# A depthwise convolution over four row tiles of 64 rows and one of 32 rows instead of five of 64

## The chip, the cores and the metric

The kernel runs on one core of a Trainium2 chip. The metric is the device time of one execution in microseconds. All arrays are fp32; TensorE works on them as sums of two parts (a leading and a trailing one), since one pass alone is not exact enough.

## The reference

The input is 8 images x 96 channels x 256 x 256. Layer 0 normalises, runs a windowed linear attention with two projections and a batch norm, and is added to its input. Layer 1 is what the change touches:

```python
x = x + _L0_conv_ref(_gn(x), ...)          # attention
x = x + _L1_conv_ref(_gn(x), ...)          # wavelet convolution
# _L1_conv_ref, B, C, H, W = 8, 96, 256, 256
for i in range(3):
    co = haar2d(cur)                       # (B, C, 4, h, w), h = H / 2, H / 4, H / 8
    cur = co[:, :, 0]
    flat = dwconv(flat, wconv_w[i]) * wscale[i]        # 5 x 5, one filter for each channel and band
for i in reversed(range(3)):
    next_ll = ihaar2d(level_coeffs[i] with next_ll added to band 0)
base = dwconv(x, base_w) * base_scale + base_b         # 5 x 5, one filter for each channel
return base + next_ll
```

## The kernel before

The program has three stages: statistics of the first image, the attention, and from about 5570 us on the wavelet convolution, which is the only stage that the change touches (but for a table of filters that the first stage lays down in memory). Its work is cut into 192 groups: 96 channels, and for each channel a first group (images 0 to 3, `g` = 0) and a second one (images 4 to 7, `g` = 1).

In a group the 256 rows of an image are covered by `WINDOWS` = 5 tiles of `WROWS` = 64 rows, of which `OROWS` = 52 are output rows and 4 on each side are halo. A tile uses 128 partitions: 64 rows times two column phases (even and odd columns). The base filter and the first wavelet level are folded into one filter, so that the convolution of a tile is a product with banded matrices `mat1`: `TAPS` = 5 column shifts, each as three matmuls (leading x leading, leading x trailing, trailing x leading; `split`, L1292 to L1294) of 512 columns (4 images x 128). The sum lies in PSUM in `ps_w` of the tile. Levels 2 and 3 work on the half-size image `ll1`, which TensorE sums up from all tiles with `down_sb` (`sum_down`, L1300), and their result `next_a`, `next_b` is added into the tiles' sums with `up_sb` (L1344, L1346).

The order on each engine is written out by hand, and semaphores join them. For group `qn`:

- TensorE: convolution of tiles 0 and 1, level 3 (L1331 to L1334), level 2 (L1292 to L1294 with `in`), convolution of tiles 2, 3 and 4, then, once `next_lo` says that `next_b` is ready, six matmuls that add the upper levels, and at once the ten of `sum_down` for group `qn + 1`.
- ScalarE: copies `ps_ll` to `ll1` (L1263), the leading parts of the inputs of levels 2 and 3 (L1265, L1267), then for group `qn + 1` the normalisation `norm` (L1243, sixteen instructions, split by half of the partitions, phase and image) and `leading` (L1256, L1258: the leading part `zb` of each tile; the first and the last tile go through a mask), then copies `ps_3` and the leading part of the upper levels (L1277, L1278).
- VectorE: `finish` of tile 0 of group `qn - 1` (L1438), `make_in` (L1392, L1395: inputs of levels 2 and 3), `finish` of tile 1, `split_in` (L1402), `finish` of tiles 2 to 4, `make_x1` for group `qn + 2` (L1369: input plus scaled attention output), `trailing` for group `qn + 1` (L1382, L1385: the trailing part of each tile, after `leading` of the same tile), `up_levels` (L1409 to L1419), `split_next` (L1424, L1426).
- GpSimd builds the banded matrices of a channel from the loaded rows: `mat1` (casts L1185, subtractions L1193) as soon as they have landed, and `mat2`, `mat3` when level 2 of the channel before has been done (`l2_ready`).
- SyncE issues all transfers in one queue: the inputs `xb`, `yb` three groups ahead, once `make_x1` has set the buffers free; the outputs, tile by tile; and behind the outputs of a channel's last group the filters `raw1`, `raw2`, `raw3` for the next channel but one, then the next inputs.

## Time and profile before

| | us |
|---|---|
| median of 3 runs | 11053.4 (11053.02 to 11074.61) |
| the profiled execution, its own time | 11061.64 |
| its span, first to last instruction | 11059.8 |
| TensorE busy in the span | 10538.7 (95%) |
| VectorE busy | 9242.7 (84%) |
| ScalarE busy | 7168.6 (65%) |
| GpSimd busy | 3679.7 (33%) |
| mean granted clock of TensorE | 0.992 of full speed |

The share of busy time is an average over three stages. The third stage repeats one pattern of two groups; the page's 40 slices show TensorE at 9 tenths in all of them, VectorE at 7, ScalarE at 5, GpSimd at 2 and the DMA engines at 7. Which engine ends a group is seen only in the timelines of single groups.

### The profile page before, as it was taken

Reading aid. Unit: us, or ns where it says so; the run is one execution under the profiler, and the core shown is the slowest. Engines: PE = TensorE matmul, PEld = TensorE weight load, DVE = VectorE, ACT = ScalarE, POOL = GpSimd, SP = SyncE. Lnnn points to the kernel's source line nnn. Section 1 sums busy time; section 2 is a strip of 40 time slices with the busy share of each in tenths; the row PEclk is TensorE's granted clock in tenths of the full one; section 3 lists DMA queues with packets and bytes.
Section 4 is the critical chain, followed back from the end, with each engine's and each line's share of the span. In section 5 each row is a group of like instructions: output and inputs, shape, how many; then the busy total and the mean of one; then the engine's idle time right before and its main releaser. Section 6 shows DMA issues by size and latency. Waiting matters only on the chain. (4 is left out here: it accounts for less than half of the span.)

```text
span 11059.8 us, 205333 instructions
## 1 busy us (share of the span) xinstructions
PE 10538.7 (95%) x66084; PEld 8946.0 (81%) x66084; DVE 9242.7 (84%) x16479; ACT 7168.6 (65%) x11852; POOL 3679.7 (33%) x3715
## 2 busy tenths in 40 slices
PE   4999999999999999999969999999999999999999
PEld 4888888888888888888858888888888888888887
DVE  6989989899998999988867777777777777777777
ACT  4777777777777777778735555555555555555554
POOL 3444444444444444444322222222222222222222
PEclk9999999999999999999979999999999999999999
DMA  5323333232333333322257777677777767767775
GB/s 185 133 92 126 109 109 126 92 130 95 126 114 104 114 103 115 126 81 74 69 124 154 155 156 154 154 152 155 156 157 157 155 153 156 155 153 154 152 156 125
DMA packets 1162861, 1453.43 MB, mean 131 GB/s; under 512 B 215391, under 2 KB 1125023, under 8 KB 1125279
## 3 DMA queue, kind: packets, MB, share of 16 engines
q1 hardware_dynamic: 1161055, 1442.80, 51.6%
q10 hardware_dynamic: 1376, 6.13, 0.1%
q8 instruction: 119, 1.95, 0.1%
q14 instruction: 311, 2.55, 0.1%
HBM read 1040.11 MB, written 408.56 MB: 131 GB/s over the span
## 5 line engine op out<-in xcount | busy, mean ns | idle before, releaser
L1292 PE MATMUL ps_w<-zb,mat 128*128 128x512 f32 x4800 | 1925.6, 401 | 8.6
L1293 PE MATMUL ps_w<-zb,mat 128*128 128x512 f32 x4800 | 1906.4, 397 | 0.0
L1294 PE MATMUL ps_w<-zb,mat 128*128 128x512 f32 x4800 | 1904.9, 397 | 0.0
L634 POOL CAST xn_hi<-xs 96x512 fp32r<-96x512 f32 x1024 | 840.7, 821 | 3112.3 <-PE ps_qkv L659 2261.1
L1438 DVE SCALAR_TENSOR_TENSOR ob<-ps_w,prm,x 64x512 f32<-64x512 f32 x1920 | 1440.5, 750 | 515.6 <-PE ps_w L1344 476.8
L1243 ACT ACTIVATE z<-x,prm 64x384 f32<-64x384 f32 (+1 forms) x3072 | 1814.0, 662 | 58.8 <-DVE x L1369 51.1
L1185 POOL CAST mat<-raw 128x1280 fp32r<-128x1280 f32 (+1 forms) x288 | 464.7, 1631 | 3947.6 <-DMA raw<-vec 2351.3
L657 PE MATMUL ps_qkv<-wqkv_hi,xn_hi 96*128 96x288 f32 x4096 | 1388.9, 339 | 38.2 <-POOL xn_lo L636 19.9
L636 POOL TENSOR_TENSOR xn_lo<-xs,xn_hi 96x512 fp32r<-96x512 f32 x1024 | 1363.4, 1331 | 81.8
L658 PE MATMUL ps_qkv<-wqkv_lo,xn_hi 96*128 96x288 f32 x4096 | 1214.1, 296 | 0.0
L659 PE MATMUL ps_qkv<-wqkv_hi,xn_lo 96*128 96x288 f32 x4096 | 1211.8, 296 | 0.0
L584 ACT ACTIVATE tok<-ps_qkv 128x1152 f32<-128x1152 f32 x1024 | 1160.6, 1133 | 0.0
L1292 PEld LDWEIGHTS ps_w<-zb,mat 128*128 128x128 f32 x4800 | 903.0, 188 | 302.9 <-DVE ob L1438 91.0
L552 ACT ACTIVATE att<-ps_t 96x512 f32<-96x512 f32 x1024 | 608.1, 594 | 805.2 <-PE ps_t L702 805.2
L687 PE MATMUL ps_g<-tok 128*104 128x97 f32 x8192 | 947.2, 259 | 160.2 <-DVE tok L795 160.1
L1294 PEld LDWEIGHTS ps_w<-zb,mat 128*128 128x128 f32 x4800 | 901.7, 188 | 227.0
L1293 PEld LDWEIGHTS ps_w<-zb,mat 128*128 128x128 f32 x4800 | 901.6, 188 | 209.3
L679 PE MATMUL ps_num<-kv_sb,q_sb 104*128 104x104 f32 x8192 | 1062.8, 273 | 0.0
L695 PE MATMUL ps_f<-att,wp_sb 96*96 96x512 f32 x2048 | 1052.6, 594 | 6.9 <-DVE f_cur_b L176 3.1
L679 PEld LDWEIGHTS ps_num<-kv_sb,q_sb 104*128 104x128 f32 x8192 | 1018.1, 192 | 0.0
L687 PEld LDWEIGHTS ps_g<-tok 128*104 128x104 f32 x8192 | 833.6, 172 | 222.4 <-DVE tok L795 219.7
L1263 ACT ACTIVATE ll<-ps_ll 128x512 f32<-128x512 f32 x192 | 114.8, 598 | 1373.4 <-PE ps_ll L1300 1373.4
(196 smaller groups left out, 24154.1 us busy)
## 6 DMA issues: line engine op xcount, KB each, us to landing
xst<-in_x SPq DMA_DIRECT2D x96, 2048.0 KB, 13.8
xs<-in_x SPq DMA_DIRECT2D x128, 1536.0 KB, 8.9
y_scratch<-ys SPq DMA_DIRECT2D x128, 1536.0 KB, 9.5
out<-ob SPq DMA_DIRECT2D x768, 208.0 KB
xb<-in_x SPq DMA_DIRECT2D x576, 256.0 KB
yb<-y_scratch SPq DMA_DIRECT2D x576, 256.0 KB
raw<-vec SPq DMA_DIRECT2D x192, 320.0 KB, 4.2
raw<-vec SPq DMA_DIRECT2D x384, 160.0 KB, 3.9
```

The costliest lines, as they stand in the source:

```text
L584: s_.activation(tok[:, slot].rearrange("p g (t c) -> p g t c", t=3)[:, :, :, 0:C], ps_qkv[:, :, 0:3 * C].rearrange("p g (t c) -> p g t c", ...
L636: nc.gpsimd.tensor_tensor(lo, pixels(xs, k, j), hi.bitcast(F32), ALU.subtract).then_inc(xlo_ready, 1)
L657: mm(o, hi, wqkv_hi[:], start=True, stop=False)
L658: mm(o, hi, wqkv_lo[:], start=False, stop=False)
L659: last = mm(o, lo, wqkv_hi[:], start=False, stop=True)
L679: last = mm(ps_num[:, g, 0:QR], q_sb[:, slot, g * 128:(g + 1) * 128], kv_sb[:, g // 2, :], start=True, stop=True)
L687: last = mm(ps_g[0:QR, w * GW:(w + 1) * GW], tok[:, slot, g, PART:PART + QR], tok[:, slot, g, 2 * PART:2 * PART + GW], start=g % 2 == 0, s ...
L1243: last = nc.scalar.activation(z[q * WROWS:(q + 1) * WROWS, ts, b, :], x1[slot(k, g)][rows, pairs, b, q::2], ACT.Identity, scale=prm[k][row ...
L1292: mm(out_, w[HI], xx[HI], start=start, stop=False)
L1293: mm(out_, w[HI], xx[LO], start=False, stop=False)
L1294: return mm(out_, w[LO], xx[HI], start=False, stop=stop)
L1438: last = v.scalar_tensor_tensor(out=ob[p:p + WROWS, t // 2].rearrange("p b w -> p (b w)")[:, q::2], in0=ps_w[t][q * WROWS:(q + 1) * WROWS, ...
```

## The change

The five tiles are laid out anew. Four of them (0 to 3) still have 64 rows and two column phases. The tile with number `SPECIAL` = 4 has `SROWS` = 32 rows, of which 24 are output rows, and four column phases (`SPHASES`), so that it uses 128 partitions too, with a quarter of the columns (`BLOCKS` = 64 an image). Its convolution needs `STAPS` = 3 shifts instead of 5, and 256 columns instead of 512. It has a matrix of its own, `mat_s`, built from `raw_s`, which eight more DMAs load for each channel, and buffers of its own: `x1_s` (the four slots side by side in the partitions), `zn`, `zq`, `zs`. ScalarE normalises its 32 rows into `zn` and then moves each of the four phases into its partitions of `zq`. The other tiles now all lie inside the image, so the masks are gone. `sum_down` writes the half-size image in another order of columns (even ones first). The constants `down_sb` and `up_sb` are made on VectorE instead of being loaded, and only the borders of the padded buffers are set to zero, for which SyncE no longer waits.

```diff
-NV1 = 4 * TAPS * 2
+NV1 = 4 * (TAPS + 2) * 2
...
+SROWS = WROWS // 2
+SPHASES = 128 // SROWS
+STAPS = 3
+BLOCKS = W // SPHASES
+SPECIAL = WINDOWS - 1
+TILES = ((0, 0, WROWS - HALO), (WROWS - 2 * HALO, HALO, WROWS - 2 * HALO),
+         (H - 2 * WROWS + 2 * HALO, HALO, WROWS - 2 * HALO), (H - WROWS, HALO, WROWS - HALO),
+         (2 * WROWS - 4 * HALO, HALO, SROWS - 2 * HALO))
+
+
+def tile_place(t):
+
+    return (t % 2) * WROWS, t // 2, SROWS if t == SPECIAL else WROWS
...
-                                full = p1[:, ia, q, :, o, first:first + 2 * TAPS - 1:2]
+                                full = p1[:, ia, q, 1:1 + TAPS, o, first:first + 2 * TAPS - 1:2]
...
-            x1 = [sb_(f"x1_{s}", [128, PAIRW, IMGS, W]) for s in range(SLOTS)]
+            x1 = [sb_(f"x1_{s}", [128, SPECIAL // 2, IMGS, W]) for s in range(SLOTS)]
+            x1_s = sb_("x1_s", [SLOTS * SROWS, IMGS, W])
             xb = sb_("xb", [128, PAIRW, IMGS, W])
             yb = sb_("yb", [128, PAIRW, IMGS, W])
             ob = sb_("ob", [128, PAIRW, IMGS, W])
-            zb = [[sbr_(f"zb{g}_{h}", [128, WINDOWS, IMGS, ZW]) for h in range(2)] for g in range(SETS)]
+            zb = [[sbr_(f"zb{g}_{h}", [128, SPECIAL, IMGS, ZW]) for h in range(2)] for g in range(SETS)]
+            zs = [[sbr_(f"zs{g}_{h}", [128, IMGS, BLOCKS + 2]) for h in range(2)] for g in range(SETS)]
...
+            raw_s = sb_("raw_s", [128, SPHASES * STAPS, SROWS])
...
+            mat_s = [[sbr_(f"mat_s{k}_{h}", [128, STAPS, 128]) for h in range(2)] for k in range(2)]
...
+            zn = sb_("zn", [SROWS, IMGS, W])
+            zq = sb_("zq", [128, IMGS, BLOCKS])
+            ll1 = sb_("ll1", [128, 2, IMGS, HALF // 2])
...
-            NRAW = (4 + 2 + 4) * 16
+            NRAW = (4 + 8 + 2 + 4) * 16
...
-                for t_ in (xb, yb, *zb[0], *zb[1], *in2_p, in3_hl):
-                    eng.memset(t_[:].bitcast(F32), 0.0).then_inc(zeroed, 1)
-                eng.memset(zero1[:], 0.0).then_inc(zeroed, 1)
-
-            N_ZERO = 2 + 2 * SETS + 3 + 1
-
-            down_raw = ob[:, 0].rearrange("p b w -> p (b w)")[:, 0:WINDOWS * HALF].rearrange("p (t w) -> p t w", t=WINDOWS)
-            up_raw = ob[:, 1].rearrange("p b w -> p (b w)")[:, 0:WINDOWS * HALF].rearrange("p (t w) -> p t w", t=WINDOWS)
+                for t_, n, width in padded_tiles:
+                    for at in (slice(0, n), slice(width - n, width)):
+                        eng.memset(t_[:].bitcast(F32)[..., at], 0.0).then_inc(zeroed, 1)
+
+            N_ZERO = 2 * len(padded_tiles)
+            N_SET = 5 + (SPECIAL + 2) + 2 * (2 * 2 * 2 + 2 * SPHASES)
+            UPPER_AT, LOWER_AT = {0: 0, 1: 1, SPECIAL: 2}, {SPECIAL: 4, 2: 6, 3: 7}
...
-                for dst, src in ((down_raw, down), (up_raw, up), (inside_sb[:], inside)):
-                    sp.dma_start(dst, src).then_inc(const_in, 16)
...
+                    for ia in range(2):
+                        for q in range(SPHASES):
+                            first = q * SROWS + ia
+                            sp.dma_start(raw_s[first:first + SROWS - 1:2, :, :],
+                                         bass.AP(tensor=vec1.tensor,
+                                                 offset=c * (NV1 * V1) + (((2 * ia + q % 2) * (2 * TAPS + 4) + q // 2 * 2) * V1
+                                                                          + (2 + WROWS - SROWS)),
+                                                 ap=[[2, SROWS // 2], [V1, SPHASES * STAPS], [1, SROWS]])).then_inc(raw_in, 16)
...
-                sp.wait_ge(zeroed, N_ZERO)
...
-                        build([(mat1[k], raw1[:].rearrange("p (d o) m -> p d (o m)", o=2)[:, :, ::-1], "p d m -> p d m")],
+                        build([(mat1[k], raw1[:].rearrange("p (d o) m -> p d (o m)", o=2)[:, :, ::-1], "p d m -> p d m"),
+                               (mat_s[k], raw_s[:].rearrange("p (d o) m -> p d (o m)", o=SPHASES)[:, :, ::-1],
+                                "p d m -> p d m")],
...
+                    for b in range(IMGS):
+                        img = IMGS * g + b
+                        last = nc.scalar.activation(
+                            zn[:, b], x1_s[own(k, g), b], ACT.Identity,
+                            scale=prm[k][own(k, g), 2 + img:3 + img], bias=prm[k][own(k, g), 2 + B + img:3 + B + img])
+                    last.then_inc(zn_set, 1)
                     for p in range(2):
-                        ts = slice(p, WINDOWS, 2)
-                        pairs = slice(0, len(range(p, WINDOWS, 2)))
+                        ts = slice(p, SPECIAL, 2)
+                        pairs = slice(0, SPECIAL // 2)
                         rows = slice(p * WROWS, (p + 1) * WROWS)
...
+                    act.wait_ge(zn_set, m * 4 + (2 * k + g + 1))
+                    for q in range(SPHASES):
+                        last = nc.scalar.activation(zq[q * SROWS:(q + 1) * SROWS].rearrange("p b j -> p (b j)"),
+                                                    zn[:].rearrange("p b w -> p (b w)")[:, q::SPHASES], ACT.Copy)
                     last.then_inc(z_set, 1)
 
                 def leading(qn, g):
                     act.wait_ge(z_set, qn + 1)
-                    for t in range(WINDOWS):
-                        o = zb[g][HI][:, t, :, 2:2 + HALF]
-                        i = z[:, t]
-                        if t in EDGES:
-                            e = EDGES[t]
-                            nc.scalar.activation(o, i, ACT.Identity, scale=mask[:, e:e + 1], bias=zero1[:]).then_inc(z_hi, 1)
-                        else:
-                            nc.scalar.activation(o, i, ACT.Copy).then_inc(z_hi, 1)
+                    for t in range(SPECIAL):
+                        nc.scalar.activation(zb[g][HI][:, t, :, 2:2 + HALF], z[:, t], ACT.Copy).then_inc(z_hi, 1)
+                    nc.scalar.activation(zs[g][HI][:, :, 1:1 + BLOCKS], zq[:], ACT.Copy).then_inc(z_hi, 1)
...
+                    for t in range(SPECIAL):
                         for h in (HI, LO):
-                            last = mm(ps_ll[:], down_sb[:, t, :], zb[g][h][:, t, :, 2:2 + HALF], start=t + h == 0,
-                                      stop=t + h == WINDOWS)
+                            mm(ps_ll[:], down_sb[:, t, :],
+                               zb[g][h][:, t, :, 2:2 + HALF].rearrange("p b (j v) -> p v b j", v=2), start=t + h == 0, stop=False)
+                    for v in range(2):
+                        for h in (HI, LO):
+                            last = mm(ps_ll[:, v * HALF * 2:(v + 1) * HALF * 2], down_sb[:, SPECIAL + v, :], zs[g][h][:, :, 1:1 + BLOCKS], start=False,
+                                      stop=v + h == 2)
                     last.then_inc(ll_ready, 1)
...
+                        if t == SPECIAL:
+                            for d in range(STAPS):
+                                split(ps_w[t][:, 0:IMGS * BLOCKS], [mat_s[k][h][:, d, :] for h in range(2)],
+                                      [zs[g][h][:, :, d:d + BLOCKS] for h in range(2)], d == 0, False)
+                            return
...
+                        for at, half in ((UPPER_AT, next_a), (LOWER_AT, next_b)):
+                            if t == SPECIAL:
+                                for v in range(2):
+                                    last = mm(ps_w[t][:, 0:IMGS * BLOCKS], up_sb[:, at[t] + v, :], half[:, v::2], start=False,
+                                              stop=half is next_b and v == 1)
+                            elif t in at:
+                                last = mm(ps_w[t][:], up_sb[:, at[t], :], half[:], start=False, stop=True)
                         last.then_inc(win_ready, 1)
...
-                        n = 128 if 2 * i + 1 < WINDOWS else WROWS
-                        v.scalar_tensor_tensor(out=x1[slot(k, g)][0:n, i].rearrange("p b w -> p (b w)"),
+                        n = 128 if i < SPECIAL // 2 else SROWS
+                        to = x1[slot(k, g)][:, i] if i < SPECIAL // 2 else x1_s[own(k, g)]
+                        v.scalar_tensor_tensor(out=to.rearrange("p b w -> p (b w)"),
...
-                        o = zb[g][LO][:, t, :, 2:2 + HALF]
-                        hi = zb[g][HI][:, t, :, 2:2 + HALF].bitcast(F32)
-                        if t in EDGES:
-                            e = EDGES[t]
-                            last = v.scalar_tensor_tensor(out=o, in0=z[:, t], scalar=mask[:, e:e + 1], in1=hi,
-                                                          op0=ALU.mult, op1=ALU.subtract)
+                        if t == SPECIAL:
+                            inner = [zs[g][h][:, :, 1:1 + BLOCKS] for h in range(2)]
                         else:
-                            last = v.tensor_tensor(o, z[:, t], hi, ALU.subtract)
-                        last.then_inc(z_lo, 1)
+                            inner = [zb[g][h][:, t, :, 2:2 + HALF] for h in range(2)]
+                        v.tensor_tensor(inner[LO], zq[:] if t == SPECIAL else z[:, t], inner[HI].bitcast(F32), ALU.subtract
...
-                        v.tensor_tensor(in2[:, s], ll1[:, :, 0::2], ll1[:, :, 1::2], op).then_inc(in2_ready, 1)
+                        v.tensor_tensor(in2[:, s], ll1[:, 0], ll1[:, 1], op).then_inc(in2_ready, 1)
...
+                        for q in range(SPHASES if t == SPECIAL else 0):
+                            last = v.scalar_tensor_tensor(
+                                out=ob[0:SROWS, t // 2].rearrange("p b w -> p (b w)")[:, q::SPHASES],
+                                in0=ps_w[t][q * SROWS:(q + 1) * SROWS, 0:IMGS * BLOCKS], scalar=prm[k][own(k, g), 1:2],
+                                in1=x1_s[own(k, g)].rearrange("p b w -> p (b w)")[:, q::SPHASES],
+                                op0=ALU.add, op1=ALU.add)
+                        for q in range(0 if t == SPECIAL else 2):
```

ScalarE, one group in the middle of the third stage: from the copy of `ps_ll` to that of the upper levels. Before:

```order
L1263 ACTIVATE ll1<-ps_ll 128x512
L1265 ACTIVATE in2_0<-in2 128x8x64
L1267 ACTIVATE in3_hl<-in3 128x8x32
L1243 ACTIVATE z<-x1_2,prm_1 64x3x128 x8
L1243 ACTIVATE z<-x1_2,prm_1 64x2x128 x8
L1256 ACTIVATE zb0_0<-z,zero1,mask 128x4x128
L1258 ACTIVATE zb0_0<-z 128x4x128 x3
L1256 ACTIVATE zb0_0<-z,zero1,mask 128x4x128
L1273 ACTIVATE s3<-ps_3 128x512
L1277 ACTIVATE next_a<-next_ll 64x512
L1278 ACTIVATE next_b<-next_ll 64x512
```

and now:

```order
L1298 ACTIVATE ll1<-ps_ll 128x512
L1300 ACTIVATE in2_0<-in2 128x8x64
L1302 ACTIVATE in3_hl<-in3 128x8x32
L1268 ACTIVATE zn<-x1_s,prm_1 32x256 x4
L1279 ACTIVATE z<-x1_2,prm_1 64x2x128 x16
L1285 ACTIVATE zq<-zn 32x256 x4
L1292 ACTIVATE zb0_0<-z 128x4x128 x4
L1293 ACTIVATE zs0_0<-zq 128x4x64
L1308 ACTIVATE s3<-ps_3 128x512
L1312 ACTIVATE next_a<-next_ll 64x512
L1313 ACTIVATE next_b<-next_ll 64x512
```

The sixteen instructions of `norm` are still there, all in the smaller form; four stand ahead of them and four behind them, and `leading` follows.

GpSimd, the matrices of one channel. Before:

```order
L1185 CAST mat1_1_0<-raw1 128x640
L1187 REGISTER_ALU
L1193 TENSOR_TENSOR mat1_1_1<-raw1,mat1_1_0 128x256 x2
L1193 TENSOR_TENSOR mat1_1_1<-raw1,mat1_1_0 128x128
L1205 REGISTER_ALU
L1185 CAST mat2_0<-raw2 128x1280
L1185 CAST mat3_0<-raw3 128x1280
L1193 TENSOR_TENSOR mat2_1<-raw2,mat2_0 128x256 x5
L1193 TENSOR_TENSOR mat3_1<-raw3,mat3_0 128x256 x5
```

and now (tile names as in the program, with the number of the channel's buffer):

```order
L1215 CAST mat1_1_0<-raw1 128x640
L1215 CAST mat_s1_0<-raw_s 128x384
L1217 REGISTER_ALU
L1223 TENSOR_TENSOR mat1_1_1<-raw1,mat1_1_0 128x256 x2
L1223 TENSOR_TENSOR mat1_1_1<-raw1,mat1_1_0 128x128
L1223 TENSOR_TENSOR mat_s1_1<-raw_s,mat_s1_0 128x256
L1223 TENSOR_TENSOR mat_s1_1<-raw_s,mat_s1_0 128x128
L1237 REGISTER_ALU
L1215 CAST mat2_0<-raw2 128x1280
L1215 CAST mat3_0<-raw3 128x1280
L1223 TENSOR_TENSOR mat2_1<-raw2,mat2_0 128x256 x5
L1223 TENSOR_TENSOR mat3_1<-raw3,mat3_0 128x256 x5
```

A cast and two subtractions for `mat_s` have come in, between the matrix `mat1` and the matrices `mat2` and `mat3`.

SyncE's queue, the filters of one channel, four kinds of DMA with their counts, now:

```order
L1133 DMA raw1<-vec1 32x10x64 x4
L1140 DMA raw_s<-vec1 16x12x32 x8
L1146 DMA raw2<-vec2 64x10x128 x2
L1150 DMA raw3<-vec3 32x10x128 x4
```

The second line is new; the inputs `xb` and `yb` of the next group to be loaded are issued behind these.

## Rows read from the trace of the kernel before

**Rows 1.** Timeline of TensorE: start us, us busy, instruction, shape, count.

```profile
8038.00 0.39 PE L1292 MATMUL ps_w<-zb,mat 128*128 128x512 f32 x1
...
8041.28 0.39 PE L1294 MATMUL ps_w<-zb,mat 128*128 128x512 f32 x1
...
8047.73 0.28 PE L1292 MATMUL ps<-in,mat 128*128 128x256 f32 x1
...
8051.40 0.39 PE L1292 MATMUL ps_w<-zb,mat 128*128 128x512 f32 x1
...
8090.32 0.86 PE L1344 MATMUL ps_w<-next_a,up_sb 128*128 128x512 f32 x3
```

**Rows 2.** Timeline of ScalarE, 8040 to 8045 us.

```profile
8040.16 0.41 ACT L1267 ACTIVATE in_hl<-in 128x256 fp32r<-128x256 f32 x1
8040.47 5.19 ACT L1243 ACTIVATE z<-x,prm 64x384 f32<-64x384 f32 x8
```

**Rows 3.** Timeline of ScalarE, 8034 to 8096 us; idle time and releaser in brackets.

```profile
8038.20 0.60 ACT L1263 ACTIVATE ll<-ps_ll 128x512 f32<-128x512 f32 x1 [8.35 <-PE ps_ll L1300]
...
8066.52 0.60 ACT L1263 ACTIVATE ll<-ps_ll 128x512 f32<-128x512 f32 x1 [5.88 <-PE ps_ll L1300]
...
8068.80 9.50 ACT L1243 ACTIVATE z<-x,prm 64x384 f32<-64x384 f32 x16
8078.34 0.82 ACT L1256 ACTIVATE zb<-z,zero,mask 128x512 fp32r<-128x512 f32 x1
8079.06 1.66 ACT L1258 ACTIVATE zb<-z 128x512 fp32r<-128x512 f32 x3
...
8094.29 0.60 ACT L1263 ACTIVATE ll<-ps_ll 128x512 f32<-128x512 f32 x1 [8.38 <-PE ps_ll L1300]
```

**Rows 4.** Timeline of VectorE, first group of a channel.

```profile
8075.62 3.66 DVE L1369 SCALAR_TENSOR_TENSOR x<-yb,gain,xb 128x1024 f32<-128x1024 f32 x3
8079.20 0.74 DVE L1382 SCALAR_TENSOR_TENSOR zb<-z,mask,zb 128x512 fp32r<-128x512 f32 x1
8079.87 1.88 DVE L1385 TENSOR_TENSOR zb<-z,zb 128x512 fp32r<-128x512 f32 x3
8081.68 0.74 DVE L1382 SCALAR_TENSOR_TENSOR zb<-z,mask,zb 128x512 fp32r<-128x512 f32 x1
...
8085.99 0.69 DVE L1426 TENSOR_TENSOR next_b<-next_ll,next_b 64x512 fp32r<-64x512 f32 x1
```

**Rows 5.** Timeline of VectorE, second group of a channel.

```profile
8050.87 0.74 DVE L1382 SCALAR_TENSOR_TENSOR zb<-z,mask,zb 128x512 fp32r<-128x512 f32 x1
...
8053.34 1.75 DVE L1382 SCALAR_TENSOR_TENSOR zb<-z,mask,zb 128x512 fp32r<-128x512 f32 x1
...
8061.24 1.13 DVE L1426 TENSOR_TENSOR next_b<-next_ll,next_b 64x512 fp32r<-64x512 f32 x1
```

**Rows 6.** Timeline of GpSimd over the same two groups.

```profile
8051.73 4.48 POOL L1185 CAST mat<-raw 128x1280 fp32r<-128x1280 f32 x2 [17.42 <-PE ps L1294]
8056.39 7.95 POOL L1193 TENSOR_TENSOR mat<-raw,mat 128x256 fp32r<-128x256 f32 x10 [0.18 <-POOL mat L1185]
8087.84 0.72 POOL L1185 CAST mat<-raw 128x640 fp32r<-128x640 f32 x1 [23.50 <-DMA raw<-vec]
```

**Rows 7.** Timeline of SyncE's queue: issues of DMAs.

```profile
8076.94 3.02 SPq L1111 DMA_DIRECT2D raw<-vec  x4
...
8084.81 0.36 SPq L1130 DMA_DIRECT2D xb<-in_x  x1
```

**Rows 8.** Windows: stretch, its length, busy us of PE, PEld, DVE, ACT, POOL (instructions), clock, DMA share, GB/s.

```profile
1480.00:1484.00 4.00, 0.69 (x5) 0.47 (x4) 1.45 (x4) 1.22 (x3) 0.00 (x0) 0.86 0.06 14
1484.00:1487.30 3.30, 3.30 (x16) 3.26 (x16) 0.98 (x2) 0.32 (x1) 0.00 (x0) 0.50 0.00 0
...
8100.00:8101.00 1.00, 1.00 (x6) 0.77 (x6) 0.97 (x2) 1.00 (x2) 0.00 (x0) 1.00 0.31 108
```

**Rows 9.** Timeline of GpSimd, and of SyncE's queue, where the third stage begins.

```profile
5569.57 2.66 POOL L1075 MEMSET xb<- 128x3072 f32 x1 [69.52 <-POOLq L885]
...
5586.53 2.73 SPq L1111 DMA_DIRECT2D raw<-vec  x4
```

More of the change, by code:

```diff
@@ new lines, in _ @@
+                dve.wait_ge(down_set, 5)
+                for t, (start, skip, n) in enumerate(TILES):
+                    to = slice((start + skip) // 2, (start + skip + n) // 2)
+                    for v_ in range(2 if t == SPECIAL else 1):
+                        first = skip // 2 + v_ * (SROWS // 2)
+                        v.tensor_scalar(down_sb[:, t + v_, to], pair_sums[:, t // SPECIAL, first:first + n // 2], 0.5, None,
+                                        ALU.mult).then_inc(down_set, 1)
@@ new lines, in _ @@
+                for rows, at in ((0, UPPER_AT), (64, LOWER_AT)):
+                    for t in at:
+                        start, skip, n = TILES[t]
+                        width = tile_place(t)[2]
+                        src = ident_sb[rows:rows + 64, (start + skip) // 2:(start + skip + n) // 2]
+                        for q in range(128 // width):
+                            which = at[t] + (q // 2 if t == SPECIAL else 0)
+                            for to in (0, 64):
+                                o = up_sb[to:to + 64, which, q * width + skip:q * width + skip + n]
+                                v.tensor_scalar(o.rearrange("p (a r) -> p a r", r=2), src.unsqueeze(2).to_broadcast(
+                                    [64, n // 2, 2]), 0.5, None, ALU.mult).then_inc(down_set, 1)
```

86 lines of the change are left out of this document (40 added, 46 removed).

## The prediction

> **What bounds the kernel now.** The page puts TensorE at 95%, which would make it the bound. I read the timelines of the single engines over the two groups of one channel, since the shares cannot tell who is late at the end of a group. Each group is measured from the copy of `ps_ll` on ScalarE (L1263), which I call T0: 8038.20 for a second group, 8066.52 for the next first group, 8094.29 for the one after [rows 3]. So a second group takes 28.32 us and a first group 27.77, and the pair 56.09.
>
> In the first group TensorE ends it. VectorE has `next_b` ready at 8085.99 + 0.69 = 8086.68, T0 + 20.16 [rows 4], and TensorE comes to the upper levels only at 8090.32, T0 + 23.80 [rows 1]. VectorE is 3.6 us early. In the second group VectorE ends it: `next_b` is ready at 8061.24 + 1.13 = 8062.37, T0 + 24.17 [rows 5], later than TensorE's 23.8. From there six matmuls, `sum_down` and the semaphores take 4.15 us to the next T0.
>
> Why does VectorE take 4 us more in the second group? From the start of `trailing` to the end of `next_b` it needs 7.48 us in the first group (8079.20 to 8086.68) and 11.50 in the second (8050.87 to 8062.37) [rows 4, 5]. The work is the same, but GpSimd builds `mat2` and `mat3` meanwhile, from 8051.73 to 8064.34 [rows 6]; the same instruction on the last tile takes 0.74 us in the one group and 1.75 in the other. The Trainium skill (SBUF — State Buffer, "Who interferes with whom") says that a VectorE instruction with two SBUF inputs and a GpSimd instruction that reads SBUF exclude one another for their whole length, and that the one which starts second is blocked. These two rows agree with it.
>
> The third near tie is ScalarE. In the first group `norm` runs from 8068.80 for 9.50 us and the first leading part is there at 8078.34 + 0.82 = 8079.16 [rows 3]. VectorE comes out of `make_x1` and starts `trailing` at 8079.20 [rows 4]. There is no slack at all between them.
>
> **TensorE saves.** Fifteen matmuls of 512 columns in tile 4 become nine of 256. The pace is (8041.28 - 8038.00) / 14 = 0.234 us for the large and (8051.40 - 8047.73) / 30 = 0.122 for the small ones [rows 1]: 3.51 - 1.10 = 2.41 us a group. The columns of the upper levels and of `sum_down` stay the same in sum. TensorE would now be ready at T0 + 21.39. What `sum_down` pays for reading every second column no row shows; the bounds are nothing and a doubling of eight matmuls (1.9 us a group, on the path in both groups). I take nothing, since the elements moved are as many.
>
> **ScalarE pays.** The larger form of `norm` costs 5.19 / 8 = 0.65 us, the smaller one (9.50 - 5.19) / 8 = 0.54 [rows 2, 3]. Sixteen small ones make 8.62. Four for `zn` at the small form's price, which has the same per-partition scale and as many elements, make 2.16 (bounds 0.41 and 0.54 each). Four for `zq`, plain copies of 256 elements, are nearest to L1267's 0.41 [rows 2]: 1.64 (0.54 each as the upper bound). `norm` is then 12.42 us, 2.92 more. The first leading part becomes a plain copy, 1.66 / 3 = 0.55 and about 0.2 cheaper than the masked one with its overlap [rows 3]. So `trailing` can start 2.72 us later than now, at T0 + 15.40 instead of T0 + 12.68. The copies for `zq` read every fourth fp32. By the same page of the Trainium skill (its note on cachelines) a stride of two still hits a 16-byte line twice and a stride of four does not, so that `zq` should cost extra; no row here shows it.
>
> **VectorE.** `finish` of tile 4 gets four instructions of 256 instead of two of 512; each has a fixed part, and I reckon 0.5 us more. That lies ahead of `make_x1` and under ScalarE's delay. `trailing` gets four at 0.6 and one at half of that, 2.74 us instead of 3.14 (the two masked ones 0.67 each): 0.40 less [rows 4]. From `trailing` to `next_b` it is 7.48 - 0.40 = 7.08.
>
> **First group.** `next_b` at 15.40 + 7.08 = T0 + 22.48, later than TensorE's 21.39. VectorE's chain takes over, and of TensorE's 2.41 us only a part comes through: 22.48 + 4.15 = 26.63, against 27.77 now: -1.14.
>
> **Second group.** Here four things come together.
> 1. GpSimd's matrices start at the end of level 2, T0 + 13.5 (8051.73 - 8038.20), and last 12.6 us [rows 6]. Now `trailing` starts 0.9 us ahead of the first cast (8050.87), so that its first four tiles run free, and the excess is 4.0 us in all [rows 5]. Then it will start 1.9 us after the first cast, and all ten instructions with two SBUF inputs meet GpSimd. I reckon 4.5 (bounds 4.0, as now, and 6.0: ten times the 0.5 to 0.6 which the later ones lose, plus half a cast).
> 2. The filters. Eight DMAs of 192 short rows stand in SyncE's queue between the old ones and the inputs. An issue takes 0.36 to 0.76 us [rows 7]; at 0.55 that is 4.4 us. The matrices `mat1` started at 8087.84, T0 + 21.3 of the first group, while VectorE stood idle [rows 6]. They will start near T0 + 26 and, with `mat_s`, lie over `make_in` of the second group, which delays ScalarE's start as well. The inputs are issued from 8084.81 [rows 7] and the DMA engines were busy with them up to about 8100 [rows 8], T0 + 5.7 of the second group; `make_x1` wants them at T0 + 9.1 (as 8075.62 in rows 4). They will land near T0 + 11.6. `make_x1` then ends near T0 + 15 or 16. For both together I take 1.0 us (bounds 0 and 1.7).
> 3. `next_b` comes at 15.40 + 1.0 + 7.08 + 4.5 = T0 + 27.98. TensorE, ready at 21.4 to 23, stands idle for 5 us or more.
> 4. In the attention stage TensorE was busy for 0.69 of 4.0 us (1480 to 1484), and the granted clock in the next 3.3 us of full work was 0.50, the 1.2 GHz level [rows 8]. So the upper levels and `sum_down`, which end the path, can run at half pace: nothing to 3 us, and I take 1.5. The Trainium skill (TensorE: Matmul & The Clock Gate, "HAM oscillation") warns of idle gaps in each round of a loop in the same sense.
>
> Sum: 15.40 + 1.0 + 7.08 + 4.5 + 4.15 + 1.5 = 33.63 against 28.32: +5.31.
>
> **Sum.** The pair costs 5.31 - 1.14 = +4.17 us, times 96 channels = +400. At the start of the stage SyncE no longer waits for the memsets (from 5569.57 to 5586.53 [rows 9]), 17.0 us, less 4.4 for the new issues: -12. The constants made on VectorE lie beside this load. Together +388. Against the profiled execution's 11061.6 that is 11450; the median of the runs lies 8.2 us below it, so I forecast 11441, rounded to 11440.
>
> **The rivals.**
> - *Data come in time and the clock holds.* Then the second group is 15.40 + 7.08 + 4.5 + 4.15 = 31.1, +2.8, the pair +1.7, with the start +150: 11200. With the cheapest ends (4.0 for GpSimd, `zn` at 0.41) it is about +60. For it: 5 us of idle may miss the clock. Chance 0.22.
> - *The inputs come so late that `make_x1` runs under GpSimd's casts.* Its three instructions of 1.2 us have two SBUF inputs each; at the 1.0 us that a blocked one lost [rows 5] the second group gets 3 us more: +288, 11730. Strided reads of `sum_down` would add in the same range (1.9 x 192 = 365). For it: the inputs' landing at T0 + 11.6 is only 2 us ahead of the casts. Chance 0.14.
> - *Faster: ScalarE's delay is swallowed in the second group.* If GpSimd and VectorE, after the shift, exclude one another no longer than now and the new eight small ScalarE instructions cost half of my price (0.24 each), the second group stays near 28.3 and the first gains 2.4: -230 - 12, 10810. It decides at a second group of under 29.5 us. Against it: 0.41 is the cheapest 256-element instruction in these rows. Chance 0.12.
> - *No change.* The losses and gains cancel between these. Chance 0.04.
>
> **How the numbers follow.** My forecast, VectorE's chain late in both groups with the clock falling in the second, has 0.48. The range leaves out the faster case and the far half of the late inputs: 11090 to 11720. For a change of under 0.2% (22 us) a measurement of this kernel cannot tell it from none. Slower: 0.48 + 0.22 + 0.14 = 0.84, of which 0.01 goes to the middle for the cheapest ends; same 0.05; faster 0.12.
>
> **What the profile after would show.** TensorE's matmuls of tile 4 at 0.12; `norm` of 24 instructions at 12.4 us; VectorE waiting 2 us for ScalarE ahead of `trailing` in both groups, where it waited for nothing; T0 distances near 26.6 and 33.6; GpSimd's `mat1` cast after the next T0; the clock below 1.0 every 60 us. I am wrong if ScalarE's new instructions are cheap, if VectorE is in time under GpSimd, or if the clock stays full.

## The result, and the profile after

The changed kernel takes 11952.8 us (median of 4; 11946.8 to 11959.9) against 11053.7 before: ratio 1.081, 95% interval 1.079 to 1.083. It is slower, as forecast, but by 899 us instead of 387, and outside the range. The profiled execution has a span of 11954.6 us, and 0.955 as TensorE's mean granted clock instead of 0.992.

The page of the changed kernel, engines' busy time:

```profile
PE 10633.6 (89%) x65700; PEld 8937.1 (75%) x65700; DVE 9509.9 (80%) x16897; ACT 7811.3 (65%) x13388; POOL 3825.1 (32%) x4015
```

TensorE has 384 matmuls fewer and is busy for 95 us longer, and its share falls from 95% to 89%. So its busy time did not fall with the number of matmuls and columns.

ScalarE's timeline of the two groups, which answers to [rows 3]; a second group is 8035.35 to 8071.01, a first one 8071.01 to 8101.05:

```profile
8035.35 0.60 ACT L1298 ACTIVATE ll<-ps_ll 128x512 f32<-128x512 f32 x1 [7.10 <-PE ps_ll L1338]
...
8071.01 0.60 ACT L1298 ACTIVATE ll<-ps_ll 128x512 f32<-128x512 f32 x1 [7.97 <-PE ps_ll L1338]
...
8073.41 2.06 ACT L1268 ACTIVATE zn<-x_s,prm 32x256 f32<-32x256 f32 x4
8075.50 8.59 ACT L1279 ACTIVATE z<-x,prm 64x256 f32<-64x256 f32 x16
8084.10 2.67 ACT L1285 ACTIVATE zq<-zn 32x256 f32<-32x256 f32 x4
8086.80 2.20 ACT L1292 ACTIVATE zb<-z 128x512 fp32r<-128x512 f32 x4
...
8101.05 0.60 ACT L1298 ACTIVATE ll<-ps_ll 128x512 f32<-128x512 f32 x1 [7.26 <-PE ps_ll L1338]
```

The pair takes 65.70 us; it took 56.09. (Averages over all 96 channels are in the table at the end of the experiments; this pair is typical of them.) `norm` is 2.06 + 8.59 + 2.67 = 13.3 us, and the four copies for `zq` take 0.67 each, half as much again as my 0.41.

VectorE in the first group [rows 4] and, below the gap of the timeline, in the second [rows 5]:

```profile
8078.67 2.72 DVE L1480 SCALAR_TENSOR_TENSOR ob<-ps_w,prm,x_s 32x256 f32<-32x256 f32 x4
...
8083.82 1.27 DVE L1414 SCALAR_TENSOR_TENSOR x_s<-yb,gain,xb 32x1024 f32<-32x1024 f32 x1
8087.47 2.50 DVE L1427 TENSOR_TENSOR zb<-z,zb 128x512 fp32r<-128x512 f32 x4 [2.38 <-ACT zb L1292]
...
8093.88 0.69 DVE L1468 TENSOR_TENSOR next_b<-next_ll,next_b 64x512 fp32r<-64x512 f32 x1
```

```profile
8035.98 1.30 DVE L1434 TENSOR_TENSOR in<-ll 128x256 f32<-128x256 f32 x2 [4.70 <-ACT ll L1298]
8037.31 1.18 DVE L1437 TENSOR_TENSOR in<-in 128x128 f32<-128x128 f32 x2
...
8053.08 4.12 DVE L1427 TENSOR_TENSOR zb<-z,zb 128x512 fp32r<-128x512 f32 x4 [2.44 <-ACT zb L1292]
...
8063.11 0.69 DVE L1468 TENSOR_TENSOR next_b<-next_ll,next_b 64x512 fp32r<-64x512 f32 x1
```

In both groups `trailing` (L1427) now waits 2.4 us for ScalarE (L1292). `finish` of the special tile (L1480) takes 2.7 us. In the second group `make_in` takes 1.30 and 1.18 us where the first has 0.76 and 0.49, since GpSimd's `mat1` and `mat_s` lie over it, and `trailing` takes 4.12 us instead of 2.50 under GpSimd's casts and subtractions. GpSimd's timeline, which answers to [rows 6]:

```profile
8033.97 0.72 POOL L1215 CAST mat<-raw 128x640 fp32r<-128x640 f32 x1 [37.15 <-DMA raw<-vec]
8034.63 0.51 POOL L1215 CAST mat_s<-raw_s 128x384 fp32r<-128x384 f32 x1
...
8050.09 2.87 POOL L1215 CAST mat<-raw 128x1280 fp32r<-128x1280 f32 x2 [11.29 <-PE ps L1328]
8053.15 9.21 POOL L1223 TENSOR_TENSOR mat<-raw,mat 128x256 fp32r<-128x256 f32 x10 [0.18 <-POOL mat L1215]
```

TensorE, from the upper levels to the end of `sum_down` (L1334), second group and first group, which answers to the last of [rows 1]:

```profile
8063.86 1.22 PE L1391 MATMUL ps_w<-next_a,up_sb 128*128 128x512 f32 x2 [5.78 <-DVE next_b L1468]
...
8066.65 3.83 PE L1334 MATMUL ps_ll<-zb,down_sb 128*128 128x512 f32 x8
```

```profile
8094.62 0.73 PE L1391 MATMUL ps_w<-next_a,up_sb 128*128 128x512 f32 x2 [2.09 <-DVE next_b L1468]
...
8096.71 3.82 PE L1334 MATMUL ps_ll<-zb,down_sb 128*128 128x512 f32 x8
```

TensorE waits 5.8 us for VectorE in the second and 2.1 in the first group. The eight matmuls of `sum_down` then take 3.65 us to the start of the next row of work (8066.65 to 8070.30, 8096.71 to 8100.35), 0.456 each. In the kernel before, the ten of the same size took 2.37 us (8091.72 to 8094.09), 0.237 each:

```profile
8091.72 2.53 PE L1300 MATMUL ps_ll<-zb,down_sb 128*128 128x512 f32 x10
```

The windows show what TensorE was granted there (columns as in [rows 8]):

```profile
8064.00:8067.00 3.00, 3.00 (x9) 2.58 (x10) 1.50 (x2) 0.00 (x0) 0.00 (x0) 0.50 0.00 0
8067.00:8071.00 4.00, 4.00 (x13) 2.39 (x12) 0.00 (x0) 0.00 (x0) 0.00 (x0) 0.86 0.22 61
8095.00:8098.00 3.00, 3.00 (x11) 2.46 (x10) 1.50 (x2) 0.00 (x0) 0.00 (x0) 0.58 1.08 302
8098.00:8101.00 3.00, 3.00 (x11) 1.89 (x10) 0.00 (x0) 0.00 (x0) 0.80 (x2) 0.85 0.99 223
```

The clock had fallen in both groups, even after the gap of 2.1 us. (Over the stage it was low at the end of every second group and of two first groups in three.) So these windows cannot say whether `sum_down` is slow for its stride or for the clock. Over the whole stage the trace leans to the stride: the large matmuls of `sum_down` that lie wholly in stretches of full clock take 0.456 us as well. What each costs, the experiments say.

Step by step, in us (T0 is the copy of `ps_ll`):

| | forecast, first | measured | forecast, second | measured |
|---|---|---|---|---|
| T0 to the start of `trailing` | 15.40 | 16.46 | 16.40 | 17.73 |
| to the end of `next_b` | 7.08 | 7.10 | 11.58 | 10.72 |
| to the next T0 | 4.15 | 6.48 | 5.65 | 7.21 |
| group | 26.63 | 30.04 | 33.63 | 35.66 |

### The profile page after: what moved, and what is told of

It is laid out like the page before. It is cut to its first block, busy times and chain, and to the rows that moved or that the text cites. A ratio compares the mean times of both kernels' runs of the same rounds, so it can differ in the third digit from the quotient of the medians.

```text
span 11954.6 us, 209320 instructions
## 1 busy us (share of the span) xinstructions
PE 10633.6 (89%) x65700; PEld 8937.1 (75%) x65700; DVE 9509.9 (80%) x16897; ACT 7811.3 (65%) x13388; POOL 3825.1 (32%) x4015
## 4 chain that ended last, share of the span: by engine, by line
ACT 24%; DVE 13%; PE 11%; issue 5%; SPq 0%; DMA 0%; DVEq 0%; ACTq 0%
ACT z L1279 13%; PE ps_ll L1334 6%; ACT zq L1285 4%; DVE zb L1427 4%; ACT zn L1268 3%; PE ps_w L1391 3%; PE ps_w L1388 1%; DVE in L1434 1%; ACT zb L1292 1%; DVE next_b L1468 1%; DVE next_a L1466 1%; ACT next_a L1312 1%; DVE sum L1451 1%; ACT ll L1298 1%; DVE zs L1427 1%
## 5 line engine op out<-in xcount | busy, mean ns | idle before, releaser
L1215 POOL CAST mat<-raw 128x1280 fp32r<-128x1280 f32 (+1 forms) x288 | 348.0, 1226 | 4686.6 <-DMA raw<-vec 3597.9
L1326 PE MATMUL ps_w<-zb,mat 128*128 128x512 f32 x3840 | 1550.9, 404 | 132.1 <-DVE ob L1486 128.6
L1279 ACT ACTIVATE z<-x,prm 64x256 f32<-64x256 f32 x3072 | 1640.8, 605 | 11.5
L1328 PE MATMUL ps_w<-zb,mat 128*128 128x512 f32 x3840 | 1531.0, 399 | 0.0
L1327 PE MATMUL ps_w<-zb,mat 128*128 128x512 f32 x3840 | 1530.9, 399 | 0.0
L1486 DVE SCALAR_TENSOR_TENSOR ob<-ps_w,prm,x 64x512 f32<-64x512 f32 x1536 | 1152.6, 750 | 203.4 <-PE ps_w L1391 173.7
L1223 POOL TENSOR_TENSOR mat<-raw,mat 128x256 fp32r<-128x256 f32 (+1 forms) x1248 | 1070.4, 891 | 34.7 <-POOL mat_s L1215 17.4
L1326 PEld LDWEIGHTS ps_w<-zb,mat 128*128 128x128 f32 x3840 | 725.2, 189 | 371.6 <-DVE ob L1486 214.1
L1427 DVE TENSOR_TENSOR zb<-z,zb 128x512 fp32r<-128x512 f32 x768 | 648.3, 905 | 437.2 <-ACT zb L1292 437.2
```

What stands on the lines that cost most here:

```text
L1279: last = nc.scalar.activation(z[q * WROWS:(q + 1) * WROWS, ts, b, :], x1[slot(k, g)][rows, pairs, b, q::2], ACT.Identity, scale=prm[k][row ...
L1326: mm(out_, w[HI], xx[HI], start=start, stop=False)
L1327: mm(out_, w[HI], xx[LO], start=False, stop=False)
L1328: return mm(out_, w[LO], xx[HI], start=False, stop=stop)
L1427: v.tensor_tensor(inner[LO], zq[:] if t == SPECIAL else z[:, t], inner[HI].bitcast(F32), ALU.subtract).then_inc(z_lo, 1)
```

## The experiments

Four theories stood after the result: the stride of `sum_down`; the clock fallen in the gaps; ScalarE's longer `norm`; the new filters. They are not exclusive; the question is what each costs, and whether they add up.

**e1: sum_down without a stride.**

```diff
-   zb[g][h][:, t, :, 2:2 + HALF].rearrange("p b (j v) -> p v b j", v=2)
+   zb[g][h][:, t, :, 2:2 + HALF]
```

> The changed kernel with the eight large matmuls of sum_down reading zb in the order in which it lies, as before the change, and ll1 with interleaved columns again. The four small matmuls of the special tile still write their 256 columns side by side, so that they add into the wrong columns: this leaves the special tile's share of the half-size image out of place. Theory 1 (a moving operand with every second fp32 is read at half the pace): the pace goes from 0.46 us a matmul back to 0.24, 1.8 us less a group on the path that ends both groups, 192 groups: about -340 us, 11610. Theory 2 (these matmuls are slow only because TensorE's clock has fallen in the gap ahead of them): the pace stays near 0.46 in the window at the 1.2 GHz level and the time stays near 11950.

Measured: 11742.6 us, -210. TensorE, first group:

```profile
8015.42 0.73 PE L1390 MATMUL ps_w<-next_a,up_sb 128*128 128x512 f32 x2 [2.10 <-DVE next_b L1467]
...
8017.36 3.33 PE L1334 MATMUL ps_ll<-zb,down_sb 128*128 128x512 f32 x8
```

The eight take 3.17 us up to 8020.53, 0.40 each: not 0.24, though the stride is gone. Their clock was 0.63 of full speed (8018 to 8021). Neither theory holds alone. Over the whole stage the large matmuls of e1 take 0.238 us where the clock is full and 0.427 where it is at its low level, 0.33 on average; (0.456 - 0.33) x 8 x 192 = 194 us is nearly all of the 210.

**e2: the stride alone, in the kernel before.**

```diff
-   zb[g][h][:, t, :, 2:2 + HALF]
+   zb[g][h][:, t, :, 2:2 + HALF].rearrange("p b (j v) -> p v b j", v=2)
```

> The kernel before with one part of the change alone: sum_down reads every second column (all ten matmuls), ps_ll and ll1 have the even columns first. Theory 1 (stride halves the pace): ten matmuls at 0.46 instead of 0.24, +2.2 us in each group, 192 groups: +420 us, 11475. Theory 2 (the fallen clock): there is no gap of more than 1 us in this kernel, so the pace stays 0.24 and the time 11055.

Measured: 11479.6 us, +432 against 11047.5 (ratio 1.039, 1.037 to 1.041). The same matmuls, and the window over them:

```profile
8011.38 4.72 PE L1300 MATMUL ps_ll<-zb,down_sb 128*128 128x512 f32 x10
```

```profile
8011.40:8016.00 4.60, 4.60 (x12) 2.11 (x11) 0.62 (x1) 0.00 (x0) 0.40 (x1) 1.00 0.34 77
```

Ten matmuls run 4.6 us at a clock of 1.00. Reading every second fp32 takes nearly twice the time, with the clock at its full level. This part of the change alone costs 4% of the old kernel. The new read also goes in rows of 64 elements, but that is not the cause: the small matmuls of `sum_down` in the changed kernel read rows of 64 side by side at 0.12 us for 256 columns, while those of the upper levels, whose only peculiarity is the step of two (`half[:, v::2]`), take 0.22 to 0.24.

**e3: the copies for zq without their stride.**

```diff
-   zn[:].rearrange("p b w -> p (b w)")[:, q::SPHASES]
+   zn[:].rearrange("p b w -> p (b w)")[:, q * W:(q + 1) * W]
```

> The changed kernel with the four copies into zq reading 256 contiguous elements instead of every fourth: this leaves the phases of the special tile unseparated. Theory: the stride of 16 bytes makes each copy 0.67 us instead of about 0.41, ScalarE's norm is on the path in both groups, so 1.0 us less a group, 192 groups: -200 us, 11750. Rival: the cost is that of a small copy on 32 partitions whatever its stride, or ScalarE is not on the path: 11950.

Measured: 11819.1 us, -134, where the forecast was -200.

```profile
8010.98 0.60 ACT L1298 ACTIVATE ll<-ps_ll 128x512 f32<-128x512 f32 x1 [7.97 <-PE ps_ll L1338]
...
8024.10 1.70 ACT L1285 ACTIVATE zq<-zn 32x256 f32<-32x256 f32 x4
...
8039.94 0.60 ACT L1298 ACTIVATE ll<-ps_ll 128x512 f32<-128x512 f32 x1 [7.11 <-PE ps_ll L1338]
```

The copies take 0.43 each, as forecast for the contiguous form, and the first group falls from 30.04 to 28.96. That is the whole 1.0 us. The rest of the gain, 134 / 96 - 1.1 = 0.3 us, is the second group's. There `trailing` starts 1.0 us earlier too (T0 + 16.7 instead of 17.7 on average), but it still starts behind GpSimd's first cast and takes longer, so that `next_b` is ready only 0.2 us earlier.

**e4: the filters once.**

```diff
-   load_raw(c): raw1 x4, raw_s x8, raw2 x2, raw3 x4; build([mat1, mat_s])
+   load_raw(c): raw1 x4, raw2 x2, raw3 x4; build([mat1]); raw_s and mat_s ahead of the loop
```

> The changed kernel with raw_s loaded once, for channel 0, and mat_s built once into both buffers: this leaves out the special tile's own filter for all other channels, and with it the eight DMAs and the GpSimd work for each channel. Theory (both delay the second group: the matrices are built over make_in, which is blocked for 1.3 us, and the inputs land late): second group about 1.3 us shorter, 96 times: -125 us, 11830; more, -200, if the shorter gap also keeps the clock up. Rival (hidden behind ScalarE and its norm): within 30 us of 11950.

Measured: 11861.2 us, -92. `make_in` of the second group is back at 0.76 and 0.49:

```profile
7998.69 0.76 DVE L1439 TENSOR_TENSOR in<-ll 128x256 f32<-128x256 f32 x2 [4.71 <-ACT ll L1302]
7999.49 0.49 DVE L1442 TENSOR_TENSOR in<-in 128x128 f32<-128x128 f32 x2
```

That is 1.2 us, and 92 / 96 = 0.96 us is what comes out. The forecast was 125 us: the theory holds in size for the second group, which is 1.4 us shorter on average, and misses that the first becomes 0.4 us longer. There GpSimd's cast of `mat1`, no longer delayed by the eight DMAs, now lies over `split_next`:

```profile
8054.99 0.96 POOL L1216 CAST mat<-raw 128x640 fp32r<-128x640 f32 x1 [31.14 <-DMA raw<-vec]
```

```profile
8055.38 1.11 DVE L1473 TENSOR_TENSOR next_b<-next_ll,next_b 64x512 fp32r<-64x512 f32 x1
```

The second of these took 0.69 us in the changed kernel.

**e5 and e6: TensorE kept busy in its gap**, without and with the stride.

```diff
+   for _ in range(7 if g == 0 else 20):     # ahead of pe.wait_ge(next_lo, qn + 1)
+       mm(ps_w[SPECIAL][:, IMGS * BLOCKS:], down_sb[:, 0, :], zb[g][HI][:, 0, 0:2, 2:2 + HALF], start=False, stop=False)
+       mm(ps_w[SPECIAL][:, IMGS * BLOCKS:], down_sb[:, 0, :], zb[g][HI][:, 0, 2:4, 2:2 + HALF], start=False, stop=False)
```

> The kernel of e1 (sum_down reading without a stride; the special tile's share of the half-size image out of place), and the wait of TensorE ahead of the upper levels filled with matmuls whose result nobody reads: 14 of 256 columns in a first group (1.7 us), 40 in a second one (5.0 us). Theory (e1 gained only 210 of the 340 us because the clock had fallen in the gap, where a large matmul takes 0.4 to 0.45 us with or without a stride): the clock stays at full speed, sum_down runs at 0.24, the time from next_b to the next copy of ps_ll falls from 5.9 and 6.3 us to about 4.6 in both groups: -2.9 us a pair, 96 pairs, -280 us against e1, 11460. Rival (e1's pace is held down by something else than the clock, or the fillers only delay): 11740 or more.

> The changed kernel with the same fillers, the strided sum_down left in. Theory (stride and fallen clock each bring a matmul to about 0.45 us, and do not add up): sum_down stays at 0.46, only the six matmuls of the upper levels gain, 0.5 us in a first and 1.0 to 1.3 in a second group: -100 to -170 us, about 11820. Rival (they add up): the gain is as large as in e5, -280, 11670.

Measured: e5 11576.7 us (mean clock 0.989), e6 11863.2 us (0.992). `sum_down` in e5 and in e6, both in windows at a clock of 1.00:

```profile
8024.56 2.09 PE L1334 MATMUL ps_ll<-zb,down_sb 128*128 128x512 f32 x8
```

```profile
8028.50 3.83 PE L1334 MATMUL ps_ll<-zb,down_sb 128*128 128x512 f32 x8
```

The four kernels make a table (us):

| | stride | no stride |
|---|---|---|
| clock falls | 11953 | 11743 (e1) |
| clock held | 11863 (e6) | 11577 (e5) |

Holding the clock gains 90 us with the stride and 166 without; taking the stride away gains 210 with the fallen clock and 286 with the full one. A matmul of 512 columns takes 0.456 us when it is strided (e6, full clock), 0.427 when it runs at the 1.2 GHz level (e1) and 0.456 when it is both (the changed kernel). The two do not add up, so each hides a part of the other. Together they are 376 us. In e6 the clock was full at the end of every group; in e5 it was still low at the end of one second group in five, so that the 166 and 286 are a little small. My expectation for e5 (11460) was too low by 117. The time from `next_b` to the next T0 did fall to 4.6 us in the first groups, as forecast, and to 4.9 in the second; but the 5.9 and 6.3 us of e1 that I started from were those of a single pair, and its averages are 5.3 and 6.1. In both kernels the four small matmuls of the upper levels read `half[:, v::2]`, and stay at 0.22 to 0.24 us instead of 0.12.

**e7 and e8: the upper levels ahead of trailing**, with and without the stride.

```diff
-   make_x1; trailing(qn + 1); up_levels(qn); split_next(qn)         # VectorE
+   make_x1; up_levels(qn); split_next(qn); trailing(qn + 1)
-   norm(qn + 1); leading(qn + 1); copy of ps_3; next_a, next_b      # ScalarE
+   norm(qn + 1), the copy of ps_3 in its middle; next_a, next_b; leading(qn + 1)
```

> The changed kernel, complete and with its strided sum_down, in another order: ScalarE copies ps_3 in the middle of norm and the upper levels' leading parts before leading, VectorE does up_levels and split_next before trailing. Theory (VectorE's wait for ScalarE's longer norm, 2.4 us in both groups, is the start of the loss, and the work behind it need not wait for it): TensorE finds next_b ready and ends the first group, 21.4 + 1.9 + 4.5 = 27.8 us instead of 30.0; the second is ended by trailing at about 27, then sum_down: 31.5 instead of 35.7. [...] -6.3 us a pair: -600 us, 11350. Rival (ScalarE's chain as a whole is the bound, whatever the order): less than 150 us gained, 11800.

> e7 with the unstrided sum_down of e1 (the special tile's share of the half-size image out of place): what the new tiles would give if the reads had no stride. Theory: since the clock now stays up, the whole 1.8 us a group comes back: -340 us against e7, about 11010, level with the kernel before. Rival (something else ends the groups by then): less than 150 us less than e7.

Measured: e7 11534.2 us, -419 where -600 was forecast; e8 11277.8 us, where 11010 was. e7 computes the whole of the reference; e8, like e1, leaves the special tile's share of the half-size image out of place. In e7 the first group is 27.55 us:

```profile
8033.22 0.60 ACT L1300 ACTIVATE ll<-ps_ll 128x512 f32<-128x512 f32 x1 [8.38 <-PE ps_ll L1346]
...
8060.77 0.60 ACT L1300 ACTIVATE ll<-ps_ll 128x512 f32<-128x512 f32 x1 [6.39 <-PE ps_ll L1346]
```

The forecast was 27.8 for it, and 31.5 for the second. That one takes 33.9, and there VectorE waits for something that it had not waited for:

```profile
8012.09 2.48 DVE L1422 SCALAR_TENSOR_TENSOR x<-yb,gain,xb 128x1024 f32<-128x1024 f32 x2 [0.98 <-DMA yb<-y_scratch]
8014.60 2.16 DVE L1422 SCALAR_TENSOR_TENSOR x_s<-yb,gain,xb 32x1024 f32<-32x1024 f32 x1
```

```profile
8028.81 3.48 DVE L1421 SCALAR_TENSOR_TENSOR x<-yb,gain,xb 128x1024 f32<-128x1024 f32 x2 [3.91 <-DMA yb<-y_scratch]
```

`make_x1` waits for its inputs, 0.98 us in e7 and 3.91 in e8. They stand behind the filters in SyncE's queue, and `make_x1` then runs under GpSimd's casts (2.16 us for the third instruction instead of 1.27). The rival with late inputs, which did not show in the changed kernel, appears as the rest gets faster: `make_x1` waits for its inputs in 27 second groups of e1 and 62 of e5, mostly hidden behind ScalarE, and in nearly all of them in e7 and e8. That the filters cause it is not shown alone. What speaks for it is e10 below, which loads them once: its first groups are as short as those of e8, and `make_x1` of its second groups starts at T0 + 10.4 on average, against 14.5 in e8.

The clock did not stay up either, as the expectation for e8 had it: it was low at the end of every second group of e7 and e8. The stride's 1.8 us come back in the first groups of e8 (27.6 to 25.8), and 0.8 us in the second (33.8 to 33.0). The 256 us between e7 and e8 lie between the theory (340) and the rival (under 150).

**e9: the same order in the kernel before.**

```diff
-   make_x1; trailing(qn + 1); up_levels(qn); split_next(qn)         # VectorE
+   make_x1; up_levels(qn); split_next(qn); trailing(qn + 1)
-   norm(qn + 1); leading(qn + 1); copy of ps_3; next_a, next_b      # ScalarE
+   norm(qn + 1); copy of ps_3; next_a, next_b; leading(qn + 1)
```

> The kernel before, complete, in the order of e7: ScalarE copies ps_3 right behind norm and the upper levels' leading parts before leading, VectorE does up_levels and split_next before trailing. Theory (in the kernel before only the second group is ended by VectorE, by 0.4 us; the upper levels' six matmuls would then lie beside trailing): first group unchanged at 27.8 us, second 0.1 to 0.4 shorter: -10 to -40 us, about 11030. Rival (VectorE's work as a whole, blocked by GpSimd, ends the group whatever the order, and leading now starts later): same or up to 50 us slower.

Measured: 10981.1 us against 11061.9 (ratio 0.993, 0.991 to 0.994), the best complete kernel of the study. The rival is refuted: both groups are now ended by TensorE, 27.77 and 27.79 us. The gain is twice the upper end of the theory's 10 to 40 us.

```profile
8003.54 0.60 ACT L1263 ACTIVATE ll<-ps_ll 128x512 f32<-128x512 f32 x1 [8.36 <-PE ps_ll L1305]
...
8031.31 0.60 ACT L1263 ACTIVATE ll<-ps_ll 128x512 f32<-128x512 f32 x1 [8.40 <-PE ps_ll L1305]
...
8059.10 0.60 ACT L1263 ACTIVATE ll<-ps_ll 128x512 f32<-128x512 f32 x1 [8.42 <-PE ps_ll L1305]
```

The second group of the prediction's rows was 28.32, but that one was short for its kind: over the 96 channels of the same trace they run from 28.3 to 29.4 us and average 28.61, the first ones 27.74. In e9 both average 27.76, so that 0.85 x 96 = 82 us a kernel is the whole gain. `next_b` is ready at T0 + 24.5 on average in those second groups, not at the 24.2 of the one pair.

**e10 and e11: what is left without ScalarE's work for the special tile, and then without three of four instructions in finish.** Both stand on `sum_down` without its stride and on filters loaded once. e10 also has 24 small matmuls ahead of TensorE's wait in each second group, as in e5; e11 has none.

```diff
-   4 x zn, 4 x zq for each group
+   4 x zn, 4 x zq for the very first group of the kernel only                # e10, e11
-   for q in range(SPHASES if t == SPECIAL else 0):
+   for q in range(1 if t == SPECIAL else 0):                                 # e11
```

> The changed kernel without stride in sum_down, filters loaded once, 24 filler matmuls of 256 columns in a second group alone, and without the eight ScalarE instructions for zn and zq (the special tile of every group works on the numbers of the first one). Theory (with ScalarE no longer late, trailing starts behind make_x1 at T0 + 14.1, since finish of the special tile takes 2.7 us instead of 1.5): first group ended by TensorE near 26.0 us (27.8 before the change); second near 31.0 (28.3), since trailing starts behind GpSimd's first cast instead of ahead of it: 11150. Rival (VectorE's blocking by GpSimd does not depend on when trailing starts): second near 29.5, 11000.

> e10 without the fillers, and with one instruction instead of four in finish of the special tile (three quarters of that tile's output are left out). Theory: trailing starts at T0 + 12.1, ahead of GpSimd's first cast as before the change, VectorE loses 4 us again and not 5 or 6, and has next_b ready at T0 + 23.2: second group 27.8, first 25.9: 10850. Rival (the place of trailing against GpSimd does not matter): only the 2.0 us of VectorE's work in the second group, -190 us against e10.

Measured: e10 11253.7 us (forecast 11150), e11 10869.3 us (forecast 10850). `trailing` in a second group of e10, in a first one of e10, and in a second one of e11:

```profile
8013.99 5.58 DVE L1438 TENSOR_TENSOR zb<-z,zb 128x512 fp32r<-128x512 f32 x4
...
8046.39 2.48 DVE L1438 TENSOR_TENSOR zb<-z,zb 128x512 fp32r<-128x512 f32 x4
```

```profile
8012.36 3.55 DVE L1433 TENSOR_TENSOR zb<-z,zb 128x512 fp32r<-128x512 f32 x4
```

In e10 the first group is 25.8 us, ended by TensorE, and there the fewer columns show at last: 1.9 us less than before the change, the 2.4 us less what the strided matmuls of the upper levels cost (it is 28.16 in e5, with the same `sum_down` and ScalarE's work). The second is 32.5, worse than my 31.0: `trailing` starts at T0 + 14.1, behind the start of GpSimd's casts, and its four large instructions take 5.6 us instead of 2.5. With 2.05 us less in `finish` it starts at T0 + 12.2, ahead of the casts, and takes 3.6. e11 gains 385 us, or 4.0 a pair, from 2.05 us less on VectorE in a second group (the first is held by TensorE). On average `trailing` starts 2.06 us earlier and the way from there to `next_b` is 1.6 us shorter. The 24 small matmuls are no part of it: they end 2.5 us before `next_b` is ready in e10. The rival, 190, is out: where `trailing` meets GpSimd doubles the price of being late.

The average length of the groups over the 96 channels, in us, from the traces:

| | first | second |
|---|---|---|
| before | 27.74 | 28.61 |
| after | 30.10 | 35.74 |
| e1 | 28.89 | 34.78 |
| e2 | 29.94 | 30.82 |
| e3 | 28.95 | 35.50 |
| e4 | 30.45 | 34.37 |
| e5 | 28.16 | 33.69 |
| e6 | 29.92 | 34.91 |
| e7 | 27.61 | 33.82 |
| e8 | 25.80 | 32.98 |
| e9 | 27.76 | 27.76 |
| e10 | 25.87 | 32.62 |
| e11 | 25.79 | 28.76 |

## Why the prediction was wrong

- **The direction and most of the mechanism held.** VectorE's chain ends both groups, ScalarE's longer `norm` delays `trailing` in both, GpSimd lengthens VectorE's way to `next_b` in the second (10.72 us instead of 7.10), and the clock is low after TensorE's gap. TensorE's saving is real (tile 4 at 0.122 us a matmul, 21.4 us to the end of its convolutions) and is worth nothing here, since the two other engines end the groups.
- **The step that failed** is the one on `sum_down`: "I take nothing, since the elements moved are as many." The other bound, a doubling of eight matmuls, is what the chip does: 0.456 instead of 0.234 us, +1.8 us in both groups. e2 shows it with this part of the change alone (+432 us for ten matmuls in 192 groups). Of the 512 us beyond the forecast, taking this stride away gives back 210 in the changed kernel (e1), and 286 where TensorE is kept busy (e6 against e5). The count of elements was no reason; no row had a strided moving operand, and a cost open between 0 and 365 us, on the path of both groups, should have widened the range to its sum with the rest. The same holds for `half[:, v::2]` (0.22 to 0.24 for 0.12 us), which I did not name at all. No run takes that stride away; the upper levels take 1.93 us at full clock in e6 and 1.40 before, and I estimate from that 0.5 us a group, some 100 us. The Trainium skill's note (SBUF — State Buffer, on cachelines), by which a stride of two fp32 still hits a line twice and is free, leans to my choice; for TensorE's operand e2 decides against it.
- **The clock** was taken for the second group alone, at 1.5 us, after gaps of 5 us. It is low in two first groups in three as well, after 2.1 us. e6 prices it at 90 us in the changed kernel, nearly all in the second groups (0.8 us each), less than my 144: strided matmuls have nothing to lose to it (0.456 us at either level).
- **zq**: priced at 0.41, 0.67 measured; 1.0 us a group on ScalarE, of which the first group gives back all and the second 0.2 to 0.3 (e3: 134 us). The rule of the Trainium skill (SBUF — State Buffer, on cachelines) that a stride of four costs extra, which I quoted and did not count, agrees with the trace.
- **Right in size:** `trailing` to `next_b` in the first group (7.08 and 7.10) and, 0.9 us too high, in the second (11.58 and 10.72); and the start of the stage, where the filters' issue begins 1.8 us after that of the parameters instead of 18.7. The filters (forecast 1.0 us a pair, e4 0.96) came out right partly by luck: a larger cost in the second group and a gain in the first, which the forecast did not have, nearly make the same sum.
- **Too small:** the issue of `raw_s`, 5.97 us for eight instead of 4.4, and `finish` of the special tile, 2.7 instead of 2.0 us, hidden in the changed kernel, decisive in e10.
- **A slip in a rival:** with the cheapest ends (0.5 us less under GpSimd, 0.5 less for `zn` in each group) the pair comes out level, and the sum near 0, not at +60 us.
- **The rivals.** Data in time and the clock held: the data did come in time, the clock did not hold. Late inputs: not in the changed kernel; they delay VectorE in e7 and e8. The faster case: refuted, ScalarE's small instructions cost 0.51 and 0.67 us, not 0.24.

## What to carry to other kernels

Read who ends a stage in each of its repeating parts before pricing a saving. In the second group VectorE was already behind TensorE, so fewer matmuls alone could bring nothing there; in the first it was 3.6 us ahead, and the change used that up. Read this from several repeats: in the one pair of the rows the second group is 0.55 us longer than the first, on average 0.9 us (e9). That a new access pattern moves as many elements does not make it free; if no row shows it, its upper bound belongs in the range, or it is tried alone in the old kernel first, as in e2. Work that nobody waits for yet (`trailing`) goes behind the work that the next engine does wait for; that order alone made the old kernel 0.7% faster.
